# The place of row statistics and expert merges in VectorE's step of two causal attentions

## The reference

```
# layer 1, self-attention with 16 heads of width 8 ("l1s" in the kernel)
att = where(tril, q @ k.T * 8 ** -0.5, -inf)
y = softmax(att) @ v
# layer 2, first attention with 16 heads of width 32 ("a1")
a = softmax(q @ k.T * 32 ** -0.5) * mask      # the mask comes after the softmax
x_out = x + (a @ v).reshape(...) @ li1_w + li1_b
```

## Time and profile before

| what | value |
|---|---|
| median of 3 runs | 2486.17 us (2484.84 to 2491.94) |
| profiled execution, its own time | 2488.64 us |
| its span | 2486.9 us |
| granted TensorE clock over the span | 0.946 of full speed |
| busy share PE, DVE, ACT, POOL | 86%, 73%, 54%, 50% |

### The profile page before, as it was taken

The page is one execution under the profiler, slowest core; times in us unless marked ns, Lnnn a source line. Parts: engine busy times, 40 slices in busy tenths (PEclk is TensorE's granted clock), DMA queues, the critical chain, the costliest instruction groups (busy, mean ns, idle before and its releaser), DMA issues. The chain is left out here.

```text
span 2486.9 us, 67321 instructions
## 1 busy us (share of the span) xinstructions
PE 2136.2 (86%) x22352; PEld 1629.6 (66%) x22352; DVE 1824.4 (73%) x4650; ACT 1335.7 (54%) x2821; POOL 1247.5 (50%) x1940
## 2 busy tenths in 40 slices
PE   5878997999988779599999997899789999998755
PEld 4557995556656568466666666666567888875523
DVE  5975554666659766489999968688698866667887
ACT  2444552444434456355555547355468888873466
POOL 4547635555535366477777745333264343334333
PEclk9978998999999879799999999899999999999978
DMA  8022211000000223200000000000000312210000
GB/s 307 20 112 76 78 53 30 16 13 14 11 2 1 83 76 105 62 13 11 9 9 11 8 2 21 10 1 0 19 5 2 103 56 67 56 43 15 1 11 24
DMA packets 82031, 96.69 MB, mean 39 GB/s; under 512 B 16720, under 2 KB 61136, under 8 KB 79760
## 3 DMA queue, kind: packets, MB, share of 16 engines
q1 hardware_dynamic: 73616, 77.12, 9.9%
q0 software_dynamic: 8192, 16.79, 2.3%
HBM read 56.51 MB, written 37.36 MB: 38 GB/s over the span
## 5 line engine op out<-in xcount | busy, mean ns | idle before, releaser
L1722 DVE TENSOR_TENSOR l2f_h_lo<-l2f_h,l2f_h_hi 128x512 fp32r<-128x512 f32 x256 | 187.1, 763 | 101.1 <-ACT l2f_h_hi L1643 101.0
L1012 POOL TENSOR_TENSOR a_pm<-a_pt,tri_post 128x256 f32<-128x256 f32 x256 | 179.6, 731 | 71.8 <-ACT a_pt L668 71.4
L1650 ACT ACTIVATE l2f_h<-l2f_f,ahead 128x512 f32<-128x512 f32 x256 | 174.2, 688 | 49.6 <-DVE l2f_h_lo L1722 32.5
L808 DVE TENSOR_REDUCE l1s_negm<-l1s_s 128x6 bf16<-128x768 f32 x128 | 123.1, 961 | 95.7 <-PE l1s_s L485 95.5
L1817 POOL TENSOR_TENSOR l2f_acc<-l2f_tmp,l2f_acc 128x512 f32<-128x512 f32 x56 | 73.0, 1303 | 207.2 <-DVE l2f_tmp L1740 207.2
L668 ACT ACTIVATE l1s_pt<-l1s_st 128x768 f32<-128x768 f32 x128 | 96.9, 812 | 144.9 <-PE l1s_st L523 144.9
L808 DVE TENSOR_REDUCE a_negm<-a_s 128x4 bf16<-128x1024 f32 x128 | 156.2, 1220 | 23.2 <-PE a_s L485 23.1
L1643 ACT ACTIVATE l2f_h_hi<-l2f_h 128x512 fp32r<-128x512 f32 x256 | 154.4, 633 | 0.0
L668 ACT ACTIVATE a_pt<-a_st 128x1024 f32<-128x1024 f32 x128 | 126.6, 1066 | 3.3 <-PE a_st L523 3.3
L684 ACT ACTIVATE a_q_hi<-a_pa 128x256 bf16<-128x256 f32 x64 | 24.5, 383 | 184.7 <-PE a_pa L451 184.7
L1534 PE MATMUL l2f_f<-l2f_x_hi,l2f_w_hi 128*128 128x512 f32 x256 | 101.7, 397 | 1.2 <-POOL l2f_w_lo L1804 1.2
(11 more groups left out here) (575 smaller groups left out, 6930.1 us busy)
## 6 DMA issues: line engine op xcount, KB each, us to landing
expert_rows<-zeros SPq DMA_DIRECT2D x16, 1056.0 KB, 17.5
l2f_wrow<-weights_by_expert SPq DMA_DIRECT2D x64, 256.0 KB, 3.2
l0f_w<-in_l0f_w SPq DMA_DIRECT2D x8, 640.0 KB, 9.7
l0f_x_in_sb<-expert_rows SPq DMA_DIRECT2D x72, 64.0 KB
expert_rows<-l0f_y SPq DMA_DIRECT2D x72, 64.0 KB, 1.6
l1f_x_in_sb<-expert_rows SPq DMA_DIRECT2D x72, 64.0 KB
expert_rows<-l1f_y SPq DMA_DIRECT2D x72, 64.0 KB
ahead<-in_l2f_w SPq DMA_DIRECT2D x6, 512.0 KB, 4.6
```

What stands on the lines that cost most here:

```text
L808: dve.tensor_reduce(dst, src, AX.X, ALU.max, negate=True).then_inc(max_done, 1)
L1012: last = pool.tensor_tensor(pm[:, par, heads_, kt, :], pt[:, par, heads_, kt * (T + P):kt * (T + P) + P], K["tri_post"][:].unsqueeze(1).br ...
L1650: act.activation(h[:, j], psum_f[j][:], ACT.Gelu, bias=col(e, j)).then_inc(h_ready, 1)
L1722: dve.tensor_tensor(h_lo[:, pos % 2, j], h[:, j], h_hi[:, pos % 2, j].bitcast(F32), ALU.subtract)\
```

## The change

A new function `norms_of(at, kinds)` holds the loop over the plan. For the attentions with `U == 4` VectorE now does only `apply` between the two maxima; the items `merge` and `stats` come at the end of its step. For `U == 1` the order stays. Nothing is added or taken away on any engine, and PE, ACT, POOL and SP keep their order.

```diff
+            def norms_of(at, kinds):
+                for when, what, i in sorted(plan, key=lambda p: (-p[0], p[2])):
+                    na, ba, ua, posa = at(LEAD - when)
+                    if inside(na) and ua == 0 and what in kinds:
+                        if what == "merge":
+                            merge_choice(ba, (posa // U) % 2, i)
+                        elif what == "stats":
+                            ln_stats(ba, i)
+                        else:
+                            ln_apply(ba, i)
...
                 if inside(nn):
                     maxima(nn, posn, 0)
-                for when, what, i in sorted(plan, key=lambda p: (-p[0], p[2])):
-                    na, ba, ua, posa = at(LEAD - when)
-                    if inside(na) and ua == 0:
-                        if what == "merge":
-                            merge_choice(ba, (posa // U) % 2, i)
-                        elif what != "gather":
-                            ln_stats(ba, i) if what == "stats" else ln_apply(ba, i)
+                norms_of(at, ("apply",) if U == 4 else ("stats", "apply"))
                 residual_now = inside(nw) and uw == U - 1 and store_t is None
                 if residual_now and inside(nn):
                     residuals(bw)
...
                         normalise(n1, n1, b1, u1)
                     elif u1 == U - 1:
                         normalise(b1, n1, b1, u1)
+                if U == 4:
+                    norms_of(at, ("merge", "stats"))
                 if residual_now and not inside(nn):
                     residuals(bw)
```

## The result

The changed kernel takes 2542.43 us (median of 4 runs, 2532.57 to 2546.05), the kernel before 2486.62 us: a ratio of 1.0215, 95% interval 1.0182 to 1.0247. The ratios in this document are those on record for the pairs of kernels, and can differ by up to 0.002 from the quotient of the two medians. The changed kernel is slower by some 56 us where 37 were forecast, and 2542 us lies above the range of 2505 to 2538. The profiled execution took 2543.14 us, 54.5 more than that of before.

What follows compares the result with a forecast made beforehand. PE was busy for 86% of 2486.9 us; l1s was taken as bound by latency, a1 by PE. Median 2486.17 plus 36.9 (l1s) plus 0 (a1) gave 2523 us, range 2505 to 2538.

Steps and rivals of the forecast that it cites:

- The side: Whole kernel: the change makes it slower, chance 0.92, against 0.04 for within 0.3% and 0.04 for faster.
- the main term: l1s: late statistics delay keys and PE's next scores by 2.77 us in twelve sequences, 36.9 us in all.
- a1: Stage a1: the period of a sequence stays, 0 us, with bounds of -9 and +9 us.
- The loop over POOL: a1: POOL's work, values to second maxima, division and statistics to veps form a loop of 26.87 us, the present period.
- Two signs: a1: POOL waits for statistics three times a sequence; the last norm's apply takes 0.7 to 1.4 us instead of 3.2.
- The rule of the Trainium skill: a1: 2-port tensor_scalar and GpSimd exclude each other; alone, it gives about 2.5 us a sequence, cut to 0.69.
- rival (5): l1s: PE's clock falls to 0.83, its 238 busy us become 287, the kernel takes 2572 us; chance 0.04.

## Why the prediction failed

**The side and the main term held.** The chain from VectorE's late statistics through POOL's queue to the keys was named with its links. Its length was worked out at 2.77 us a sequence and 36.9 us in all. With PE kept busy in the gap it measured 2.8 us a sequence and 38.1 to 38.9 us, of which some 1.3 are the writes' own. Shortening it by the gather's piece shortened PE's wait from 3.4 to 2.0 us; taking the keys out of it removed the loss.

**a1 held too.** The loop over POOL was summed to 26.87 us and the period measured 26.77; the term was 0 us, the stage gave 1.7. The loop is there in the changed kernel, piece by piece:

```profile
1280.12 0.43 PE L588 MATMUL a_nd<-a_pm,a_v_f 128*32 128x128 f32 x8 [0.55 <-POOL a_pm L1019]
...
1290.55 1.22 DVE L808 TENSOR_REDUCE a_negm<-a_s 128x4 bf16<-128x1024 f32 x1 [0.36 <-PE a_s L485]
...
1294.29 0.38 POOL L938 TENSOR_SCALAR a_veps<-a_mv 128x2 f32<-128x2 f32 x1 [0.77 <-DVE a_mv L781]
...
1303.87 2.76 POOL L1019 TENSOR_TENSOR a_pm<-a_pt,tri_post 128x256 f32<-128x256 f32 x4
...
1306.89 0.43 PE L588 MATMUL a_nd<-a_pm,a_v_f 128*32 128x128 f32 x8 [0.53 <-POOL a_pm L1019]
```

From values to maxima it is 10.43 us (10.68 in the sum), from there to veps 3.74 (2.72 + 1.08), from veps to the mask's end 12.34 (12.39), and 0.26 from there to the values, which the sum had left out. That the sum met the period to the digit was luck; its pieces are right to within 0.3 us. That the gather lies in the loop agrees with the kernel without it, which runs at 26.2 us. There the rstd's place changed as well, so how much of the 0.6 us each of the two gave is not told apart. Two signs were off: POOL waits for the statistics of a1 twice a sequence (23 times in 11), not three times, and the apply takes 0.59 us, not 0.7 to 1.4.

The rule of the Trainium skill on the shared port (SBUF — State Buffer, section Who interferes with whom) is borne out in the rows: the apply fell from 3.2 to 0.59 us once it met no mask. A merge is no tensor_scalar, but it too went from 0.35 us to as much as 2.37 beside a mask. It was right not to take the rule as the stage's gain. In the kernel before PE's weight loads of a1 did wait for VectorE's maxima, 22 times and 9.7 us in 325; with VectorE relieved, the loop over POOL holds the stage in its place.

**The step that failed is rival (5), PE's clock.** In the sum the slower clock was a term of nothing; as a rival it had a chance of 0.04, and 2572 us. The error was to weigh it by a mean: PE would be busy for 80% of l1s, nearer to a stretch at 86% with the clock at 1.00 than to one at 64% with 0.83. The mean hides how the idle lies. The 80% of l1s are work with pauses of up to 0.4 us and then one gap of 3.4 us, and late in this gap, or up to 1.3 us behind its end, the clock falls to 1.2 GHz and stays there for 3.4 or for 6.8 us. That costs 0.7 to 1.7 us a sequence: in the first profile 56.1 - 38.9 = 17 us, nearly the whole of the 17.6 us between forecast and measured profile. The same busy share with two clocks stands in the rows. PE alone, two other stretches of the kernel before:

```profile
60.00:120.00 60.00, 50.18 (x720) 1.00 0.09 35
760.00:840.00 80.00, 68.43 (x986) 1.00 0.00 1
```

l1s of the kernel with the statistics behind the join:

```profile
440.00:700.00 260.00, 218.13 (x2743) 0.94 0.05 12
```

and of the kernel with the keys first:

```profile
440.00:700.00 260.00, 223.25 (x2896) 0.97 0.05 12
```

PE is busy for 84% in the first and third of these rows and for 86% in the second and fourth. In the two of the kernel before no gap is longer than 0.7 us; in the other two there is one of up to 2.7 and up to 2.0 us once a sequence. The stretches differ in their work too; the same idle time in one piece and in several, in one stage, was not tried. I had also given the rival as all or nothing, the whole stage at 0.83, where it is an addition to the forecast: 2523 + 17 for the clock + 2 for the chain - 2 for a1 = 2540 us, against 2542 measured.

The clock as the cause is shown by the writes into the gap: the same lateness of the keys, the clock at 1.00, and the excess gone. By the size of the gap: 0.6 us of waiting left 1.00 over the stretch, 2.0 us 0.97 with falls at 4 of 14 gaps, 2.7 us 0.94 with falls at 9 of 14, 3.4 us 0.86 to 0.95 with falls at 8 to 12 of 13. What stays open is why a gap of 3.34 us passes once without a fall and one of 3.19 us does not; the length alone does not decide it in these rows, and it was not tried further. The changed kernel's runs spread over 13 us, and their times go by the granted clock over the span: 2532.57 us at 0.932, 2541.71 at 0.930, 2543.14 at 0.929, 2546.05 at 0.927.

**Chances and range.** The side had 0.92 and held. The range ended at 2538 because the clock's case stood outside it with 0.04. With the price above, 10 to 20 us on top of the forecast, it would have had to reach to 2545.

## What to carry to other kernels

An instruction with slack of several steps can still be on the critical path, if the engine that waits for it has an in-order queue: look at what stands behind the waiting instruction, and move the wait behind that work before moving what it waits for. When a change opens one long gap on PE, count the slower clock behind it as a cost of its own, and look for it at the longest gap in the timeline; here the busy share misled. Two orders on two engines may each be worth nothing or less alone (1.0215 and 1.0021 here) and 0.9969 together. But look for the smaller change as well: the merges alone, with the statistics left in place, gave 0.9970.

## What the hardware showed that I had not expected

A gap of 3.4 us once in 22 us, in a stage in which PE works all the rest of the time, is enough to bring its clock down from 2.4 to 1.2 GHz in most sequences (12 of 13 gaps in one profile, 8 of 13 in another). It stays down for 3.4 or for 6.8 us, up to some 6 of them after work has gone on. Gaps of 1.5 to 2.0 us did it too, at 4 of 14 in the kernel with keys first. A merge of 0.35 us on VectorE took 2.26 us when it began just ahead of four mask products on GpSimd that took 2.8 us in all.
